# A decoder layer on one core: value products of two units together, and row copies moved off VectorE

## What is computed

```python
x = x + attn(layernorm(x)) @ Wff.T + bff                # softmax(q k / sqrt(128)) v, 16 heads of 8
x = x + xattn(layernorm(x), ctx, mask) @ Wo.T + bo      # 77 keys, softmax(q k / sqrt(8)) v
n = layernorm(x)
gate = l2norm(n @ Wp.T) @ l2norm(sim).T / temperature
top_v, top_i = top_k(gate, 2); p = softmax(top_v)       # two experts of eight
x = x + sum_k p_k * (gelu(n @ W1[i_k] + b1[i_k]) @ W2[i_k] + b2[i_k])
```

## Time and profile before

| | us |
|---|---|
| median of three runs | 1272.8 |
| lowest and highest run | 1271.0, 1275.72 |
| the profiled execution, its own time | 1271.58 |
| its span, first to last instruction | 1269.9 |
| TensorE busy (matmul) | 1084.2 |
| VectorE, ScalarE, GpSimd busy | 886.2, 848.4, 535.1 |

### The profile page before, as it was taken

How to read it: one execution, slowest core, us unless ns; L and a number is a source line. 1 busy time by engine, 2 the same in 40 slices (tenths; PEclk the granted TensorE clock), 3 DMA queues, 4 the chain that set the end, 5 groups by cost and what they waited for, 6 DMA issues and landing times. The chain is left out here.

```text
span 1269.9 us, 32462 instructions
## 1 busy us (share of the span) xinstructions
PE 1084.2 (85%) x11795; PEld 782.0 (62%) x11795; DVE 886.2 (70%) x2617; ACT 848.4 (67%) x1729; POOL 535.1 (42%) x518
## 2 busy tenths in 40 slices
PE   2577899999999999999999999978716999999950
PEld 1345566677676667766776776645404888888740
DVE  2644657687787787787877866664365888888846
ACT  1145567777777787777777767754415999999840
POOL 4302323244444444344444434342350666666660
PEclk9867899999999999999999999998857999999985
DMA  4327484464454544634644541320064232232219
GB/s 96 85 59 161 119 176 94 105 166 100 119 142 109 135 106 118 162 95 113 163 103 119 140 103 55 100 68 28 29 223 186 80 85 79 81 82 80 71 37 374
DMA packets 119326, 144.24 MB, mean 114 GB/s; under 512 B 33944, under 2 KB 98360, under 8 KB 114240
## 3 DMA queue, kind: packets, MB, share of 16 engines
q1 hardware_dynamic: 107824, 120.37, 37.2%
q0 software_dynamic: 9168, 17.21, 4.4%
q10 hardware_dynamic: 2176, 4.59, 1.0%
HBM read 88.42 MB, written 55.36 MB: 113 GB/s over the span
## 5 line engine op out<-in xcount | busy, mean ns | idle before, releaser
L571 ACT ACTIVATE probs<-sc_a 77x512 f32<-77x512 f32 (+1 forms) x512 | 301.3, 591 | 154.9 <-PE sc_a L993 77.2
L1008 PE MATMUL pv<-probs,big 128*32 128x128 f32 x4096 | 214.0, 287 | 2.7 <-ACT probs L571 0.6
L720 DVE TENSOR_REDUCE negm_m<-sc_m 128x4 f32<-128x512 f32 x256 | 174.8, 685 | 54.3 <-PE sc_m L972 52.8
L1281 POOL DMA_INDIRECT y_d<-yo,row x156 | 161.4, 1034 | 120.4 <-issue 79.2
L720 DVE TENSOR_REDUCE negm_cm<-sc_m 128x4 f32<-128x308 f32 x256 | 119.7, 473 | 125.1 <-PE sc_m L977 103.2
L449 POOL DMA_INDIRECT xs_d<-xrow,slot_i x128 | 127.4, 996 | 154.4 <-PE sc_a L993 131.0
L1008 PEld LDWEIGHTS pv<-probs,big 128*32 128x32 f32 x4096 | 83.0, 108 | 98.3 <-issue 54.5
L1376 DVE TENSOR_TENSOR gl<-g,gh 128x512 fp32r<-128x512 f32 x156 | 107.4, 689 | 36.4 <-ACT g L1325 20.3
L972 PE MATMUL sc_m<-ks,qs 96*128 96x128 bf16 x1024 | 106.4, 232 | 29.5 <-DMA ks<-stk_k 13.8
L972 PEld LDWEIGHTS sc_m<-ks,qs 96*128 96x128 bf16 x1024 | 75.3, 103 | 76.0 <-issue 57.7
L988 PE MATMUL sc_a<-cqs,cks 102*77 102x128 bf16 x1024 | 101.0, 221 | 6.0 <-DMA cqs<-cmscr 6.0
(11 more groups left out here) (198 smaller groups left out, 2498.4 us busy)
## 6 DMA issues: line engine op xcount, KB each, us to landing
xg<-xs_d SPq DMA_DIRECT2D x39, 260.0 KB
stk_q<-parts_q SPq DMA_DIRECT2D x16, 384.0 KB, 2.5
stk_k<-parts_k SPq DMA_DIRECT2D x16, 384.0 KB
qs<-stk_q SPq DMA_DIRECT2D x16, 384.0 KB
ks<-stk_k SPq DMA_DIRECT2D x32, 192.0 KB
stk_cq<-parts_cq SPq DMA_DIRECT2D x16, 384.0 KB, 2.9
cqs<-stk_cq SPq DMA_DIRECT2D x16, 384.0 KB, 5.5
xin<-x_dram SPq DMA_DIRECT2D x16, 256.0 KB
```

Of the source, the lines that this page charges most:

```text
L571: nc.scalar.activation(probs[e % 3][0:rows], sc_a[e % 2][0:rows], ACT.Exp, scale=scale)\
L720: nc.vector.tensor_reduce(out=negm[n][:, s, g, 4 * half:4 * half + 4], in_=sc_m[u % 2][:, 0:4 * cols].rearrange("p (j k) -> p j k", j=4), ...
L1008: i = nc.tensor.matmul(pv[s % 2][32 * c:32 * c + VW, (u % 4) * S:(u % 4 + 1) * S], va[:, s, HG * g + 4 * half + c, :], probs[u % 3][:, c * ...
L1281: nc.gpsimd.indirect_dma_start(out=y12_d, in_=yo[par][:, c, :], in_offset=None, bounds_check=2 * B * S - 1, oob_is_err=False, out_offset=b ...
```

## The change

- `beside` calls `values` at even steps only, for units u - 4 and u - 3. `probs` has four buffers in place of three, and the exponential of unit e waits for unit e - 4.
- `xrow` becomes a pair of buffers. `normalise("3", ...)` writes into its first row directly, `xn_3` is gone. The copies of VectorE's `rows` are gone; a new function `twin` on GpSimd copies the first row to the second (four times 128 numbers per partition), behind `x2res` and ahead of the power.
- The second part of k is rounded by GpSimd, directly ahead of the third.
- `rest` of cq shares its buffer with q's, m's and cm's lie in k's; VectorE waits for the third parts that read them last. `sq_junk` becomes bf16. The wait for the spare tiles' stores moves from VectorE to ScalarE.

The diff, cut to its core:

```diff
@@ -143,7 +143,7 @@
-        xn = {n: sa(f"xn_{n}", [128, NS, D]) for n in ("1", "2", "3")}
+        xn = {n: sa(f"xn_{n}", [128, NS, D]) for n in ("1", "2")}
@@ -155,21 +155,22 @@
-        rest = {n: sa(f"rest_{n}", [128, T]) for n in ("q", "k", "cq")}
+        rest = {n: sa(f"rest_{n}", [128, T]) for n in ("q", "k")}
+        rest["cq"] = rest["q"]
...
-        rest["m"] = rest["cm"] = sa("rest_m", [H, T])
+        rest["m"] = rest["cm"] = rest["k"][0:H, :]
...
-        probs = [sa(f"probs{i}", [128, T]) for i in range(3)]
+        probs = [sa(f"probs{i}", [128, T]) for i in range(4)]
...
-        sq_junk = sa("sq_junk", [128, NS, D])
+        sq_junk = sa("sq_junk", [128, NS, D], BF16)
@@ -183,7 +184,7 @@
-        xrow = sa("xrow", [128, NS, 2, DW])
+        xrow = pair("xrow", [128, NS, 2, DW])
@@ -240,7 +241,7 @@
-        x3_st, rows_ok = sem("x3_st", 16), sem("rows_ok", 2)
+        x3_st, rows_ok, twin_ok = sem("x3_st", 16), sem("rows_ok"), sem("twin_ok")
@@ -438,15 +439,21 @@
-                def enlist(b, lo, hi):
+                def twin(b, row):
...
+                    pool.wait_ge(ln_ok["3"].sem, ln_ok["3"].val(b))
+                    nc.gpsimd.tensor_copy(row[:, :, 1, 0:D], row[:, :, 0, 0:D]).then_inc(twin_ok.sem, 1)
...
+                def enlist(b, row, lo, hi):
                     if lo == 0:
+                        pool.wait_ge(twin_ok.sem, twin_ok.val(b))
                         pool.wait_ge(slot_ok.sem, slot_ok.val(b))
...
                         pool.nop(nofuse=True)
-                        nc.gpsimd.indirect_dma_start(out=xs_d, in_=xrow[:, c // 2, c % 2, :], in_offset=None,
+                        nc.gpsimd.indirect_dma_start(out=xs_d, in_=row[:, c // 2, c % 2, :], in_offset=None,
                                                      out_offset=bass.IndirectOffsetOnAxis(ap=slot_i[:, c:c + 1], axis=0))\
@@ -461,31 +468,35 @@
                         residual(x2res[1 - par], x2, bo_b, x2res_ok)
+                    if on_(t - 4):
+                        twin(t - 4, xrow[par])
                     if on_(t - 3):
...
                     if on_(t + 2):
+                        pool.wait_ge(drained["k"].sem, drained["k"].val(t + 2))
+                        nc.gpsimd.tensor_copy(parts["k"][:, 1, :], rest["k"][:]).then_inc(part2["k"].sem, 1)
                         third("k", t + 2)
...
                     if on_(t - 4):
-                        enlist(t - 4, 0, 4)
+                        enlist(t - 4, xrow[par], 0, 4)
                     if on_(t + 1):
...
                     if on_(t - 4):
-                        enlist(t - 4, 4, 5)
+                        enlist(t - 4, xrow[par], 4, 5)
                     if on_(t + 3):
...
                     if on_(t - 4):
-                        enlist(t - 4, 5, 6)
+                        enlist(t - 4, xrow[par], 5, 6)
                     if on_(t - 3):
...
                     if on_(t - 4):
-                        enlist(t - 4, 6, 8)
+                        enlist(t - 4, xrow[par], 6, 8)
                     if on_(t):
@@ -556,7 +567,8 @@
                         act.wait_ge(ln_st[n].sem, ln_st[n].val(b))
-                    nc.scalar.activation(xn[n][:, s, :], src[:, s, :], ACT.Identity, bias=lnnm[n][:, s:s + 1],
+                    to = xrow[b % 2][:, s, 0, 0:D] if n == "3" else xn[n][:, s, :]
+                    nc.scalar.activation(to, src[:, s, :], ACT.Identity, bias=lnnm[n][:, s:s + 1],
                                          scale=lnrs[n][:, s:s + 1]).then_inc(ln_ok[n].sem, 1)
@@ -566,9 +578,9 @@
-                            if e >= 3:
-                                act.wait_ge(pv_ok[n].sem, pv_ok[n].val(b, e - 2))
-                            nc.scalar.activation(probs[e % 3][0:rows], sc_a[e % 2][0:rows], ACT.Exp, scale=scale)\
+                            if e >= 4:
+                                act.wait_ge(pv_ok[n].sem, pv_ok[n].val(b, e - 3))
+                            nc.scalar.activation(probs[e % 4][0:rows], sc_a[e % 2][0:rows], ACT.Exp, scale=scale)\
@@ -608,8 +620,10 @@
                         if 0 <= u < 0 + NS and on_(t - 3):
-                            if u == 0:
-                                wait_block(act, rows_ok, t - 4)
+                            if u == 0 and t - 3 == 1:
+                                act.wait_ge(fill_st.sem, 16 * (SPARE - 1))
+                            if u == 0 and t - 3 >= 1:
+                                act.wait_ge(listed.sem, listed.val(t - 5))
                             normalise("3", t - 3, x3, u - 0)
@@ -707,10 +721,6 @@
-                def second(n, b):
-                    dve.wait_ge(drained[n].sem, drained[n].val(b))
-                    nc.vector.tensor_copy(parts[n][:, 1, :], rest[n][:]).then_inc(part2[n].sem, 1)
@@ -780,12 +790,6 @@
-                    dve.wait_ge(listed.sem, listed.val(b - 1))
-                    dve.wait_ge(ln_ok["3"].sem, ln_ok["3"].val(b))
-                    for k in range(2):
-                        i = nc.vector.tensor_copy(xrow[:, :, k, 0:D], xn["3"][:])
-                    i.then_inc(rows_ok.sem, 1)
@@ -848,14 +853,16 @@
                         if u == 11 and on_(t + 2):
+                            wait_block(dve, part3["cq"], t - 1)
                             remainder("q", t + 2)
...
                         if u == 14 and on_(t + 2):
+                            wait_block(dve, part3["cm"], t - 2)
+                            wait_block(dve, part3["m"], t)
                             remainder("k", t + 2)
-                            second("k", t + 2)
                         if u == 16 and on_(t - 4):
@@ -879,6 +887,7 @@
                         if u == 18 and on_(t):
+                            wait_block(dve, part3["q"], t + 2)
                             remainder("cq", t, bq_c)
@@ -1007,7 +1016,7 @@
-                                             probs[u % 3][:, c * S:(c + 1) * S], start=True, stop=True)
+                                             probs[u % 4][:, c * S:(c + 1) * S], start=True, stop=True)
@@ -1020,7 +1029,8 @@
                                 shifted(n, b, u - LEAD, qst, kst, cols, bias)
-                            if u >= LEAD + 2:
+                            if u >= LEAD + 2 and u % 2 == 0:
+                                values(n, b, u - LEAD - 3, va, last)
                                 values(n, b, u - LEAD - 2, va, last)
```

More of the change, by code:

```diff
@@ L383, in spares @@
                     for k in range(lo, hi):
-                        sp.dma_start(spare_tile(k), xrow[:, :, 0, :]).then_inc(fill_st.sem, 16)
+                        sp.dma_start(spare_tile(k), xrow[1][:, :, 0, :]).then_inc(fill_st.sem, 16)
                 steps(sp, body, {-3: constants, 0: lambda: spares(1, 3), 1: lambda: spares(3, 5),
@@ L406, in _ @@
             def _(pool):
-                fill = xrow[:, :, 0, :]
+                fill = xrow[1][:, :, 0, :]
                 nc.gpsimd.memset(ident[:], 0.0).then_inc(ident_ok.sem, 1)
@@ L798, in weigh @@
                     dve.wait_ge(gate_step.sem, gate_step.val(b, 12))
-                    nc.vector.tensor_copy(xrow[:, :, :, D + 1], pr[:].rearrange("p k s -> p s k")).then_inc(gate_step.sem, 1)
+                    nc.vector.tensor_copy(xrow[b % 2][:, :, :, D + 1], pr[:].rearrange("p k s -> p s k")).then_inc(gate_step.sem, 1)
                 def route(b):
@@ L817, in route @@
                     dve.wait_ge(gate_step.sem, gate_step.val(b, 16))
-                    dve.wait_ge(rows_ok.sem, rows_ok.val(b, 1))
-                    nc.vector.tensor_copy(xrow[:, :, :, D].bitcast(I32), tok[:])\
+                    dve.wait_ge(rows_ok.sem, rows_ok.val(b))
+                    nc.vector.tensor_copy(xrow[b % 2][:, :, :, D].bitcast(I32), tok[:])\
                         .then_inc(gate_step.sem, 1)
@@ L841, in in_x @@
                         if u == 7 and on_(t - 2):
+                            wait_block(dve, part3["k"], t + 1)
                             remainder("cm", t - 2)
@@ L865, in in_y @@
                         if u == 7 and on_(t + 1):
+                            wait_block(dve, part3["k"], t + 2)
                             remainder("m", t + 1)
@@ L900, in gate @@
                     nc.vector.tensor_scalar(sim_u[:], sim_n[:], sim_rn[:, 0:1], None, ALU.mult).then_inc(gate_set.sem, 1)
-                steps(dve, body, {3: lambda: dve.wait_ge(fill_st.sem, 16 * (SPARE - 1)), -2: gate, -1: lambda: ones_beside(cvaug, "cv", SC)})
+                steps(dve, body, {-2: gate, -1: lambda: ones_beside(cvaug, "cv", SC)})
                 count = [0]
@@ L1099, in in_y @@
                             pe.wait_ge(ln_ok["3"].sem, ln_ok["3"].val(t - 3))
-                            transposes("x3T", t - 3, 0, [xn["3"][:, s, :] for s in range(NS)], 128)
+                            transposes("x3T", t - 3, 0, [xrow[(t - 3) % 2][:, s, 0, 0:D] for s in range(NS)], 128)
                         if u == 7 and on_(t):
```

2 lines of the change are left out of this document (1 added, 1 removed).

## The result

| | before | after |
|---|---|---|
| median of 4 runs on one chip (the three above and a fourth), us | 1273.35 | 1230.63 |
| lowest and highest | 1271.0 to 1275.72 | 1227.32 to 1231.58 |
| ratio | | 0.9678, 95% interval 0.9654 to 0.9703 |
| profiled execution / its span | 1271.58 / 1269.9 | 1227.32 / 1225.6 |

The account below looks back on a forecast made before the run. TensorE alone was taken to bind the second stage, VectorE closely with TensorE the first. Per block 1.6 + 0.75 - 0.35 + 0.05, times 16, gave 33 us: forecast 1240 us, own range 1231 to 1248, wider 1221 to 1256.

Parts of the forecast that it names:

- The price of a run: TensorE, both stages: a run of value products costs 0.09 us to enter and 0.14 to leave, whatever its length.
- Part 3 of the prediction: GpSimd rounds k's second part: `here` products end 0.3 us sooner to 0.5 later, 0 to the kernel.
- The term for products that now follow scores: TensorE, odd steps: transposes and products behind scores instead of pv gain 0.06 us at about three places a stage.
- 3 x 0.22 + 0.1 = 0.75 us is real: First stage: pairs of steps 4, 6 and 8, ahead of VectorE's unbroken stretch, save 0.75 us.
- Inside the unbroken stretch: minus 0.35: First stage: GpSimd's added row copy holds VectorE's weights' instructions, costing 0.35 us, with 0 and 0.7 as ends.
- the pairs of steps 10, 12 and 14 ... nothing: First stage: these pairs only make TensorE wait longer for the rank product L1082, gaining nothing.
- VectorE decides the first stage: First stage: VectorE never pauses from 414.64 to k's remainder at 423.08; TensorE waits 0.40 us for that.
- 16 x 2.05: Whole kernel: each stage runs 16 times, 2.05 us saved per block, 33 us in all.
- Rival (b): First stage gives back its part through copies holding 0.7 us at the weights, 0.5 at `here`: 1254 us; chance 0.17.
- Rival (c): Pairs save nothing, the entering and leaving cost hides something else that then shows: about 1271 us; chance 0.06.
- (d): Slower: pairs wait for their exponentials, TensorE stands 3.8 us a block: 1301 us; chance 0.06.
- Rival (a): VectorE does not bind the first stage, all 14 runs count, 50 us saved: 1222 us; chance 0.16.

Follow-up runs that it names:

- experiment 3: Kernel after the change with k's second part rounded by VectorE again: 1229.71 us, 0.9673 of the kernel before.
- experiment 7: Kernel after the change with GpSimd's row copy replaced by a longer product with ones: 1232.96 us, 0.9698 of the kernel before.
- Experiment 2: Kernel before the change with only the paired value products and a fourth probs buffer: 1233.12 us, 0.9703 of the kernel before.
- experiment 12: Kernel before with GpSimd's x2res residual ahead of cm's third part and VectorE's lnnm ahead of ck's remainder: 1266.74 us, ratio 0.9971.
- experiment 8: Kernel after with GpSimd's x2res residual ahead of cm's third part, VectorE's lnnm ahead of ck's remainder: 1222.82 us, 0.9650 of the kernel before.
- experiments 1: Kernel after the change without its pairs, value products one unit a step again: 1274.15 us, 1.0021 of the kernel before.
- fours: Kernel after the change with value products for four units at every fourth step and five probs buffers: 1215.99 us, 0.9603 of the kernel before.

## Why the prediction was right, and where its steps were off

**The price of a run: right.** TensorE's timelines after, at one place of a second stage and one of the first:

```profile
418.16 0.38 PE L1002 MATMUL sc_a<-identb,mbias 128*77 128x512 bf16 x1
418.38 0.30 PE L981 MATMUL sc_m<-cks,cqs 96*128 96x77 bf16 x4
...
418.88 0.38 PE L1002 MATMUL sc_a<-identb,mbias 128*77 128x512 bf16 x1
419.19 0.64 PE L1017 MATMUL pv<-probs,big 128*32 128x128 f32 x16
419.76 0.73 PE L1120 MATMUL wb<-wpx,xnT 128*128 128x136 f32 x4
```

```profile
401.97 0.39 PE L997 MATMUL sc_a<-qs,ks 102*128 102x128 bf16 x4
402.78 0.19 PE L1092 MATMUL wb<-chosen,tri 128*128 128x32 bf16 x1 [0.42 <-DVE rest_k L718]
```

L1002 takes 0.22 to the next start where scores follow and 0.31 where pv does, and two units take 0.57. A run costs 0.09 to enter and 0.14 to leave as before, and there are 14 runs a block fewer.

**Second stage: right.** 1.6 was forecast (1.54 and the small terms). Measured are 1.88 where the `here` pair lasts 1.26 us and 1.59 where it lasts 1.89, and in experiment 3, where it is short throughout, 1.81 (24.66). Part 3 of the prediction had put this pair between 0.3 us sooner and 0.5 later and at no cost in the middle; it costs 0.29 in about half the blocks. The term for products that now follow scores was too small: products in float32 that are no longer behind pv gain 0.11 (the second gate product, behind scores, takes 0.46 to the next start, the first, behind pv, 0.57), not the 0.06 that transposes gain.

**First stage: the sum was off by half, and two steps failed against each other.** Forecast: 0.75 less 0.35, that is 0.40. Measured: 0.80 in a typical block (1.29 against the one that was read, 23.69 to 22.40, above the 1 us that was named as a sign of being wrong), in these two pieces:

| first stage | before | after | less by | forecast |
|---|---|---|---|---|
| to the start of the tenth score group | 12.29 | 12.11 | 0.18 | 0.75 |
| from there to the rank product | 9.39 | 8.77 | 0.62 | -0.35 |

*"3 x 0.22 + 0.1 = 0.75 us is real"* failed. TensorE's timeline after, at the stage's beginning, and VectorE's:

```profile
383.64 0.66 PE L1047 MATMUL wb<-ident,oT 128*128 128x128 f32 x4 [0.45 <-DVE rest_q L720]
```

```profile
379.04 1.10 DVE L761 TENSOR_SCALAR gs<-graw,rn,itemp 128x8 f32<-128x8 f32 x4 [0.29 <-POOL rn L497]
...
382.15 0.75 DVE L787 TENSOR_TENSOR before<-before,chosen 128x8 bf16<-128x8 bf16 x4
382.83 0.75 DVE L720 SCALAR_TENSOR_TENSOR rest_q<-wb,bq_c,parts_cq 128x512 f32<-128x512 f32 x1
```

VectorE's choice of experts runs without a pause from 379.04 to 382.83, and the remainder of cq stands behind it. TensorE, being faster through the second stage, now comes to that place first and waits 0.45 us. Behind this wait its steps up to the tenth score group take 0.65 us less (11.02 to 10.37), which is the three runs' 0.66; before it the stage is 0.47 longer. The prediction searched for new waits inside each stage and not at the seam between them.

*"Inside the unbroken stretch: minus 0.35"* failed: it took VectorE's holds in the first stage as a given, and they moved. The rows of VectorE (which doesn't pause between them) are those under experiment 7 and these:

```profile
400.56 0.68 DVE L730 TENSOR_REDUCE negm_m<-sc_m 128x4 f32<-128x512 f32 x1
401.16 0.36 DVE L709 SCALAR_TENSOR_TENSOR lnnm<-lnmv,lnrs 128x4 f32<-128x4 f32 x1
...
402.05 0.68 DVE L718 TENSOR_TENSOR rest_k<-wb,parts_k 128x512 f32<-128x512 f32 x1
```

and beside them GpSimd:

```profile
395.83 1.26 POOL L434 TENSOR_TENSOR x2res<-x,bo_b 128x512 f32<-128x512 f32 x1
397.05 0.60 POOL L445 COPY xrow<-xrow 128x512 f32<-128x512 f32 x1
397.63 1.07 POOL L430 TENSOR_TENSOR lnrs<-lnve,mhalf 128x4 f32<-128x4 f32 x1
400.35 1.16 POOL L439 TENSOR_TENSOR parts_q<-rest_q,parts_q 128x512 bf16<-128x512 f32 x1 [1.64 <-ACT parts_q L565]
402.79 0.61 POOL L479 CAST parts_k<-rest_k 128x512 bf16<-128x512 f32 x1 [1.28 <-DVE rest_k L718]
```

lnnm ends when q's third part does (401.52 and 401.51), and lnve when the residual does (397.12 and 397.09). The same two instructions of a typical block of before, and GpSimd's third part of q beside them:

```profile
366.46 0.84 DVE L690 TENSOR_SCALAR lnve<-lnmv 128x4 f32<-128x4 f32 x1
...
371.33 0.77 DVE L695 SCALAR_TENSOR_TENSOR lnnm<-lnmv,lnrs 128x4 f32<-128x4 f32 x1
```

```profile
370.93 1.16 POOL L438 TENSOR_TENSOR parts_q<-rest_q,parts_q 128x512 bf16<-128x512 f32 x1 [2.51 <-ACT parts_q L554]
```

Holds of 0.84 + 0.77 became 0.63 + 0.36, 0.62 less, which is the whole second row of the table. The third part of q waits for ScalarE's second part. That starts right behind the remainder now (399.60 to 399.64 us); before, an evacuation of pv stood in its way, and it started 0.44 behind. GpSimd's bulk work so comes earlier against VectorE's order, and holds VectorE for less of its length: the residual starts 0.66 us ahead of lnve, and 0.45 before. That this comes from TensorE being ahead, and ScalarE's queue with it, is argued from the order of the queues. Experiment 2 shows 0.63 and 0.36 in its typical blocks (in three of the nine lnve lasts 0.83 to 0.85, in one 1.61) without any move to GpSimd: the pairs do it. The copy holds nothing here, as it takes 0.60 and not 0.89 and ends at 397.65, when the weights' instructions start. The first row of the table came out 0.57 us too low and the second 0.97 too high; that the total still lies in the range is owed in part to the two being of opposite sign.

So *"the pairs of steps 10, 12 and 14 ... nothing"* was right as to TensorE and wrong as to the stage. The wait at the rank product did grow by what they save less what VectorE gives back: from the last scores to L1092 0.81 us, where 0.23 is bare, so 0.58, against 0.19 in a typical block of before (and 0.46 in the one that was read). Some 1 us had been forecast.

**VectorE decides the first stage: right, by a hair.** In each of the ten full first stages of either kernel the rank product starts 0.73 us behind VectorE's start on the remainder of k. But experiment 12 puts TensorE's own work only 0.2 us behind that, and experiment 8 shows VectorE to be the whole bound afterwards. The one block that was read had longer holds than the others (1.05 us at lnnm, 0.77 elsewhere) and made this look firmer than it was.

**"16 x 2.05"**: the nine full blocks gave 23.0 us where the rule gives 18.5. The four thinner passes, in which values run in two first stages and four second ones, gave 7.2, where 0.40 and 1.65 a stage make 7.4. The start, with five first stages and two second ones, gave 13.3, where the same terms make 5.3. Of that, 2.2 us are there before the first scores (72.38 and 70.21), which wait for a load, and whose start differs from run to run as said. The stages' measured gains, 5 x 0.80 + 2 x 1.88, make 7.8. What is left, some 3 us, fits the clock. The stretches of the first microseconds of scores, before and then after (the granted clock is the third number from the end):

```profile
80.00:84.00 4.00, 4.00 (x44) 2.26 (x43) 1.98 (x3) 1.75 (x4) 0.00 (x0) 0.50 0.01 4
84.00:88.00 4.00, 4.00 (x41) 3.06 (x42) 1.29 (x2) 2.52 (x6) 0.00 (x0) 0.63 0.00 0
```

```profile
76.00:80.00 4.00, 4.00 (x65) 3.27 (x64) 2.58 (x4) 2.98 (x6) 0.00 (x0) 0.82 0.02 4
80.00:84.00 4.00, 4.00 (x54) 2.90 (x52) 2.26 (x4) 3.05 (x8) 0.00 (x0) 1.00 0.00 0
```

In both, TensorE comes out of some 12 us of idle time (11.85 and 12.33) at 0.50, the lower of its two levels, 1.2 GHz. Before, it is granted 2.4 GHz 14.6 us behind the first scores (at 87.0), after 7.3 us behind them (at 77.5). A score group takes 0.43 us to the next start at the lower level and 0.23 at the higher, so 7.3 us more at the lower lose 7.3 x (1 - 0.23 / 0.43) = 3.4 us, by estimate. It is not chance from run to run. In all fourteen profiles this stage starts with score groups 0.40 to 0.43 us apart, the lower level's spacing, also where a profile lists no clock for these microseconds (its stretches then print 1.00). The spacing falls to 0.23 after 14.3 to 14.6 us in the three kernels with one unit a step (before, experiments 1 and 12), and after 5.0 to 8.3 us in every kernel with pairs or fours. So the gain at the start goes with the longer runs; why the level rises sooner with them no run was made to show. Later stretches at the lower level, up to the first rank product, even some of it out: 38.5 us before and 34.6 after in all.

**The sum as a whole.** Against the 44.3 us of the spans, 32.8 was short by 11.5: by 4.6 in the nine full blocks and by 8.0 at the start, of which 3.4 are the estimate for the clock and 2.2 the earlier first scores, which differ between executions; the thinner passes gave 0.2 less than forecast, and what lies behind them 0.9 less. Rival (b) falls with the copy that holds nothing; its other half, the longer `here`, came in about half the blocks at 0.29 us. Rival (c) falls with experiments 1 and 2, (d) with the table of waits, which has one wait for probabilities. Rival (a)'s words, that "the holds fall elsewhere once TensorE's steps shift", describe what happened, but not its 50 us: VectorE binds the first stage still.

## What to carry to other kernels

Where matmuls on narrow tiles alternate with ones at full width, count the runs and not the instructions: each run cost 0.23 us here whatever its length, and it paid to buffer one more operand to make runs longer, until the neighbours' peaks took most of it back (pairs 3.2%, fours 4.0%). Before calling an engine the bound of a stage, read several repetitions of it, and the seams to the stages next to it: here the one block read was the longest of nine, and the wait that ate most of a term stood at the seam. Small VectorE instructions that happen to start inside a long GpSimd operation are worth moving by one place in either queue, if VectorE is the bound: two such moves took 0.68 us off a typical first stage after the change (the total can't be told apart by its interval) and 0.19 before it.

## What was unexpected of the hardware

GpSimd's price for one operand: the copy of 128x512 in float32 took 0.60 us and the cast of the same size to bf16 0.61, against 1.15 for the product with ones in experiment 7. The Trainium skill, GPSIMD Engine Reference, Performance versus the Vector engine, has 769 ns for 512 elements as its best case; the trace has a fifth less, and the measurement decides.

The holding of VectorE is not a slowing down: lnve and lnnm (128x4), when they come into a two operand GpSimd operation on 512 columns, end within 0.03 us of that operation's end, so that they last 0.36 or 0.84 us, whereas the reductions from PSUM beside the same operations keep their 0.68 us, and the steps of BATCH_NORM_AGGREGATE (L701) beside the residual their 0.15. Which kinds are held, and by which, was not tested further. The power of 128x4 on GpSimd, 1.07 us long at 397.63, holds none of the four weights' instructions beside it.
